# Neighbour search of an adjacency pass: three spans of 683 columns over four load slots in place of four pieces of 512

## Chip, cores and metric

One Trainium2 chip, one core. The metric is the device time of one execution in microseconds; lower is better. Three runs of the kernel before gave 4296.23, 4297.94 and 4300.20 us, median 4297.94 us. The rows below come from one more execution, taken with the profiler.

## What is computed

Four graph layers over `x` (8192 nodes, 128 features) and `adj` (8192 x 8192 float32, 256 MiB, mostly zeros: each row has a one on its own diagonal place and about eight other entries). Cut to what matters:

```
h = relu(layernorm(x));  x += relu((D^-1 A') h W0^T + b0)          # layer 0, A' from adj and alpha
h = relu(layernorm(x));  x += hyperbolic layer on adj, W1           # layer 1
h = relu(layernorm(x));  hh = h W2^T + b2                           # layer 2
                         x += max over the 32 largest entries of each row of adj of hh
h = relu(layernorm(x));  x += hyperbolic layer on adj, W3, b3       # layer 3
```

Layer 2 needs, for every row of `adj`, the columns of its 32 largest entries. A row has far fewer than 32 positive entries, so the list is all its positive columns and then the lowest-numbered zero columns.

## The kernel before, in words

The kernel reads `adj` once in its own layout. That is the adjacency pass, 16 groups (`g`) of 512 rows, each group 16 pieces (`c`) of 512 columns. A piece is 128 partitions x 4 rows x 512 columns, 1 MB, and goes to one of four slots of the SBUF tensor `PIECES`, slot `c % 4`. Each piece has three readers, on three engines:

- **TensorE (PE)** transposes it (line 526), in two pairs of 128-column blocks per piece, 32 pairs (`k`) in a group, and multiplies the transposed pair with `H` for layer 0 (line 539).
- **ScalarE (ACT)** copies each transposed pair from PSUM to one of four buffers `ATS` (line 725), and sums the piece's rows into `rs_part` (line 736). Before the first such sum of a group it waits for `rs_reduced` (line 729), which VectorE tells after its reduction of the group before.
- **VectorE (DVE)** searches it for neighbours (lines 1092 to 1106). For each of the four rows `r` the instruction `max` (MAX8) finds the eight largest values and `max_index` (a MATCH_VALUE_LOAD and a FIND_INDEX8) their places. After the 16 pieces `pick` (lines 1027 to 1086) makes of the 16 x 8 candidates of a row two lists, the near one (columns under 2048, the first four pieces) and the far one, and `L1113` adds up the row sums. If the eighth candidate of any piece is above zero, a row may have more than the search found, and line 1067 marks its tile for a slow general form, which searches the whole row again.

GpSimd's queue (POOL) stores each transposed pair, 512 KB, to the DRAM tensor `adj_turned` (line 420), so that the later layers can read the matrix transposed; pair `k` goes out after its copy and at most three stores are under way, as line 422 waits for the store two before.

The order of the loads is set by SyncE's queue (lines 323 to 332). For each piece in order it waits until the slot's old piece has been transposed (`pair_transposed`), searched (`piece_scanned`) and summed (`piece_summed`), and then issues the load (line 331). All loads of the pass stand in this one queue, in order, and each reader waits for its own slot's `piece_loaded`. The counter `piece_scanned` is raised by every MAX8 and every FIND_INDEX8, eight times per piece (`SCAN`).

After the pass come the layers 1 to 3 on the transposed copy, with gathers for layer 2 by the near and far lists (lines 433 and following). They take the same lists and the same row sums whatever way the search was made.

Of the kernel before, what the change touches and what calls it, by code (L numbers as in the profile page):

```python
# [5 lines left out]
TPG = 4  # L6
GROUP = TPG * P
PIECE = 512
SLOTS = 4
TOPK = 32  # L10
PREFIX = 64
NEAR = 4
# [17 lines left out]
ALU = mybir.AluOpType  # L30
ACT = mybir.ActivationFunctionType
AX = mybir.AxisListType
# [41 lines left out]
def build(nc, x, adj, alpha, w0, b0, w1, w2, b2, w3, b3, out):  # L74
# [3 lines left out]
    NPC = N // PIECE  # L78
    BPP = PIECE // P
    NP = NT // 2  # L80
    K4 = NPC // SLOTS
    NSG = NG // SGG
    TSG = TPG * SGG
    SGW = GROUP * SGG
# [18 lines left out]
    with ctx:  # L103
# [6 lines left out]
        def sem(name):  # L110
# [6 lines left out]
        PIECES = sb("PIECES", [P, max(SLOTS * TPG * PIECE, N)])  # L117
# [30 lines left out]
        s4 = sb("s4", [P, 10, TPG])  # L148
# [9 lines left out]
        tsc = sb("tsc", [P, 2, 6])  # L158
        eps_col = sb("eps_col", [P, 1])

        pieces = [PIECES[:, i * TPG * PIECE:(i + 1) * TPG * PIECE].rearrange("p (r x) -> p r x", r=TPG)
                  for i in range(SLOTS)]
        slot_v = [PIECES[:, i * 2 * SGW:(i + 1) * 2 * SGW].rearrange("p (b h x) -> p b h x", b=2, h=SGG)
                  for i in range(SLOTS)]
        wide = [PIECES[:, i * 2 * SGW:(i + 1) * 2 * SGW].rearrange("p (b x) -> p b x", b=2) for i in range(SLOTS)]
# [7 lines left out]
        ACC = AGG[:, :, :].rearrange("p (s r) f -> p s (r f)", r=TSG)  # L173
        DOT = H[:, :, :].rearrange("p (s r) f -> p s (r f)", r=TSG)

        CW = NPC * 8
        at = [0]

        def part(n):
# [3 lines left out]

        cand = part(TPG * CW).rearrange("p (r c e) -> p r c e", r=TPG, e=8)
        cidx = part(TPG * CW).bitcast(u32).rearrange("p (r c e) -> p r c e", r=TPG, e=8)
        cbase = part(TPG * CW).rearrange("p (r c e) -> p r c e", r=TPG, e=8)
        pos = part(TPG * CW).rearrange("p (r c e) -> p r c e", r=TPG, e=8)
        keys = part(TPG * CW).rearrange("p (r k) -> p r k", r=TPG)
        zero = part(TPG * PREFIX).rearrange("p (r k) -> p r k", r=TPG)
# [29 lines left out]
        piece_scanned = sem("piece_scanned")  # L219
# [72 lines left out]
        HALF = [slice(0, NT // 2), slice(NT // 2, NT)]  # L292
        PICK = 11 + 13 * TPG
        SCAN = 2 * TPG
        FULL_A = 16 * (1 + HALFK)
        FULL_B = 16 * HALFK
        PIECES_L1 = NSG * NP

# [14 lines left out]
        def _(sp):  # L313
# [9 lines left out]
            with sp.Fori(0, NG) as g:  # L323
                for c in range(NPC):
                    sp.wait_ge(pair_transposed, g * (2 * NPC) + 2 * (c + 1))
                    sp.sem_inc(carrier["sp"], 1)
                    sp.wait_ge(piece_scanned, g * (NPC * SCAN) + SCAN * (c + 1))
                    sp.sem_inc(carrier["sp"], 1)
                    sp.wait_ge(piece_summed, g * NPC + (c + 1))
                    sp.sem_inc(carrier["sp"], 1)  # L330
                    sp.dma_start(pieces[c % SLOTS], adj_v[bass.ds(g, 1), c, :, :, :])\
                      .then_inc(piece_loaded[c % SLOTS], 16)
# [44 lines left out]
            for c in range(CHUNKS):  # L377
                for s in range(NSG):
                    for kk in range(2):
                        n = (c * NSG + s) * 2 + kk  # L380
# [13 lines left out]
        def _(pool):  # L394
# [10 lines left out]

            pool.wait_ge(pass_ready, 1)
            pool.memset(ones, 1.0).then_inc(pick_constants, 1)
            pool.iota(cbase, [[0, TPG], [PIECE, NPC], [0, 8]], base=1, channel_multiplier=0,
                      allow_small_or_imprecise_dtypes=True).then_inc(pick_constants, 1)

            pool.sem_inc(pair_free, NAT)
# [521 lines left out]
        def _(dve):  # L933
            v = nc.vector
# [92 lines left out]
            def pick(g):  # L1027
                cf = [a.rearrange("p r c e -> p (r c e)") for a in (cand, cidx, cbase, pos)]
                kf = keys.rearrange("p r k -> p (r k)")
                posk = pos.rearrange("p r c e -> p r (c e)")  # L1030
                near, far = slice(0, NEAR * 8), slice(NEAR * 8, CW)
                lists = ((near, 0), (far, HALFK))
                pk.mark(v.tensor_tensor(kf, cf[1], cf[2], ALU.add))
                pk.mark(v.tensor_scalar(cf[3], cf[0], 0.0, None, ALU.is_gt))
# [52 lines left out]

            def scan_pass():
                with dve.Fori(0, NG) as g:
                    sc.enter(g, SCAN * NPC)  # L1090
                    pk.enter(g, PICK)
                    for c in range(NPC):
                        dve.wait_ge(piece_loaded[c % SLOTS], g * (16 * K4) + 16 * (c // SLOTS + 1))
                        dve.sem_inc(carrier["dve"], 1)
                        pc = pieces[c % SLOTS]
                        if c == 0:
                            pk.mark(v.tensor_scalar(zero, pc[:, :, 0:PREFIX], 0.0, None, ALU.is_equal))
                            pk.mark(v.tensor_reduce(s4[:, 6, :], pc[:, :, 0:PREFIX], AX.X, ALU.min))
                            pk.settle()
                        found = []  # L1100
                        for r in range(TPG + 1):
                            if r < TPG:
                                found.append(sc.mark(v.max(cand[:, r, c, :], pc[:, r, :])))  # L1103
                            if r:
                                sc.settle(found[r - 1])
                                sc.mark(v.max_index(cidx[:, r - 1, c, :], cand[:, r - 1, c, :], pc[:, r - 1, :]))  # L1106
                    sc.settle()
                    dve.wait_ge(pick_constants, 2)
                    pick(g)

                    dve.wait_ge(piece_summed, g * NPC + (NPC + SLOTS))
                    dve.sem_inc(carrier["dve"], 1)
                    pk.mark(v.tensor_reduce(tiles_of(RS[:, :], g), rs_part[:, :, :], AX.X, ALU.add))  # L1113
                    pk.settle(tell=rs_reduced)
                sc.leave(NG)
                pk.leave(NG)
# [249 lines left out]

            sc = Steps(dve, piece_scanned, carrier["dve"])
            pk = Steps(dve, pick_step, carrier["dve"])
            dve.sem_inc(piece_scanned, SCAN * SLOTS)
            dve.sem_inc(rs_reduced, 1)  # L1370
            dve.sem_inc(row_used, 1)
            link(v.memset(ones_col[:, :], 1.0))
            link(v.memset(eps_col[:, :], LN_EPS))
            sc.base = SCAN * SLOTS
            dve.wait_ge(s_load, LOADS)
            dve.wait_ge(ident_ready, 2)
            dve.wait_ge(extra_constants, 3)
# [154 lines left out]
```

## Time and profile before

| what | us |
|---|---|
| median of three runs | 4297.94 |
| lowest, highest | 4296.23, 4300.20 |
| the profiled execution, its time | 4298.19 |
| its span in the trace | 4296.5 |
| DVE busy in the span | 3633.9 (85%) |
| PE busy | 3459.1 (81%) |
| ACT busy | 1676.9 (39%) |
| POOL busy | 1639.1 (38%) |
| first search of the pass starts, last group's search starts | 91.6, 1588.9 |

The span is what the trace covers; the execution's own time is 1.7 us longer. A busy time is the sum of an engine's instructions with overlaps counted once. In the lines by group, "busy, mean ns" is followed by the idle time of the engine before these instructions and by what ended it. Durations of neighbouring VectorE instructions overlap by some tens of ns, so the pitch from start to start is shorter than the duration.

### The profile page before, as it was taken

Reading aid. Unit: us, or ns where it says so; the run is one execution under the profiler, and the core shown is the slowest. Engines: PE = TensorE matmul, PEld = TensorE weight load, DVE = VectorE, ACT = ScalarE, POOL = GpSimd, SP = SyncE. Lnnn points to the kernel's source line nnn. Section 1 sums busy time; section 2 is a strip of 40 time slices with the busy share of each in tenths; the row PEclk is TensorE's granted clock in tenths of the full one; section 3 lists DMA queues with packets and bytes.
Section 4 is the critical chain, followed back from the end, with each engine's and each line's share of the span. In section 5 each row is a group of like instructions: output and inputs, shape, how many; then the busy total and the mean of one; then the engine's idle time right before and its main releaser. Section 6 shows DMA issues by size and latency. Waiting matters only on the chain.

```text
span 4296.5 us, 52828 instructions
## 1 busy us (share of the span) xinstructions
PE 3459.1 (81%) x11588; PEld 1809.8 (42%) x11588; DVE 3633.9 (85%) x6461; ACT 1676.9 (39%) x4239; POOL 1639.1 (38%) x1850
## 2 busy tenths in 40 slices
PE   3988888898888985289998898870688978888883
PEld 3555555555555553234443343430233433333343
DVE  6999999999999999777777888882689999999964
ACT  2777777777767774300210302222111111111134
POOL 0111111111111111000037677764777777777600
PEclk9999999999999997689999999985799989999985
DMA  3988988998888985168788798881688888888841
GB/s 113 347 345 333 348 340 341 342 344 340 335 323 323 333 339 209 39 236 298 268 311 296 270 335 285 295 278 38 194 282 303 308 290 293 297 300 297 297 163 39
DMA packets 569318, 1189.00 MB, mean 277 GB/s; under 512 B 45133, under 2 KB 87054, under 8 KB 569038
## 3 DMA queue, kind: packets, MB, share of 16 engines
q1 hardware_dynamic: 426160, 818.40, 53.7%
q0 software_dynamic: 116096, 355.32, 22.5%
q10 hardware_dynamic: 26782, 12.62, 1.0%
q14 instruction: 237, 1.94, 0.1%
q8 instruction: 43, 0.70, 0.1%
HBM read 905.12 MB, written 281.05 MB: 276 GB/s over the span
## 4 chain that ended last, share of the span: by engine, by line
DVE 40%; issue 25%; POOL 13%; PE 12%; DMA 4%; ACT 3%; DVEq 2%; POOLq 1%; SPq 0%; ACTq 0%
POOL D L433 13%; DVE D L1103 12%; PE psT L600 7%; DVE D L1106 6%; DVE H L1354 4%; DMA D<-h_table,idx_now 4%; DVE ATS L1329 2%; DVE gmax L1150 2%; DVE AGG L1365 1%; PE psT L654 1%; ACT junk_rows L754 1%; DVEq L56 1%; DVE D L1052 1%; DVE sm L977 1%; DVE D L1057 1%
## 5 line engine op out<-in xcount | busy, mean ns | idle before, releaser
L433 POOL DMA_INDIRECT D<-h_table,idx_now x1324 | 1362.4, 1029 | 1022.6 <-issue 972.8
L539 PE MATMUL psU<-ATS,H 128*128 128x512 f32 x2048 | 1006.8, 617 | 123.7 <-ACT ATS L725 123.6
L600 PE MATMUL psT<-PIECES,H 128*128 128x512 f32 x2048 | 926.6, 611 | 88.1 <-DMA PIECES<-adj_turned 55.9
L654 PE MATMUL psT<-PIECES,ATS 128*128 128x512 f32 x1376 | 640.8, 621 | 191.3 <-ACT ATS L842 155.4
L420 POOL DMA_DIRECT2D adj_turned<-ATS x512 | 272.6, 532 | 1303.6 <-ACT ATS L725 846.3
L1106 DVE FIND_INDEX8 D<-D,PIECES 128x8 uint32<-128x512 f32 x1024 | 695.6, 686 | 0.0
L1329 DVE SCALAR_TENSOR_TENSOR ATS<-PIECES,dots,ATS 128x1024 f32<-128x1024 f32 x496 | 611.6, 1286 | 82.6 <-DMA PIECES<-adj_turned 75.6
L1103 DVE MAX8 D<-PIECES 128x8 f32<-128x512 f32 x1024 | 670.6, 676 | 2.3
L1354 DVE SCALAR_TENSOR_TENSOR H<-PIECES,DINV,H 128x1024 f32<-128x1024 f32 x504 | 647.4, 1287 | 29.6 <-DMA PIECES<-adj_turned 7.4
L600 PEld LDWEIGHTS psT<-PIECES,H 128*128 128x128 f32 x2048 | 393.8, 196 | 595.0 <-issue 459.1
L725 ACT ACTIVATE ATS<-psT 128x1024 f32<-128x1024 f32 x512 | 520.4, 1023 | 312.7 <-PE psT L526 162.1
L526 PEld LDWEIGHTS psT<-ident,PIECES 128*128 128x128 f32 x4096 | 488.5, 144 | 307.5 <-issue 232.8
L526 PE MATMUL psT<-ident,PIECES 128*128 128x128 f32 x4096 | 545.1, 278 | 27.8 <-DMA PIECES<-in_adj 26.2
L539 PEld LDWEIGHTS psU<-ATS,H 128*128 128x128 f32 x2048 | 362.0, 197 | 398.9 <-issue 337.4
L654 PEld LDWEIGHTS psT<-PIECES,ATS 128*128 128x128 f32 x1376 | 268.7, 199 | 545.4 <-issue 359.7
L654 PE MATMUL psU<-PIECES,ATS 128*128 128x512 f32 x672 | 317.0, 625 | 63.2 <-ACT ATS L842 32.3
L736 ACT ACTIVATE psX<-PIECES 128x512 f32<-128x512 f32 x512 | 303.6, 593 | 82.6 <-DVEq L58 82.6
L1150 DVE TENSOR_REDUCE gmax<-D 128x128 f32<-128x1664 f32 (+3 forms) x64 | 207.7, 3245 | 127.0 <-DMA D<-h_table,idx_now 126.2
L736 ACT ACTIVATE psY<-PIECES 128x512 f32<-128x512 f32 x512 | 301.3, 588 | 0.0
L842 ACT ACTIVATE ATS<-xc,tsc 128x128 f32<-128x128 f32 x64 | 25.7, 402 | 579.1 <-DVE tsc L1208 579.1
L654 PEld LDWEIGHTS psU<-PIECES,ATS 128*128 128x128 f32 x672 | 132.9, 202 | 236.4 <-issue 188.9
L761 ACT ACTIVATE ATS<-psT 128x1024 f32<-128x1024 f32 x8 | 8.2, 1023 | 489.8 <-PE psT L600 489.0
(268 smaller groups left out, 2197.5 us busy)
## 6 DMA issues: line engine op xcount, KB each, us to landing
PIECES<-adj_turned SPq DMA_DIRECT2D x512, 1024.0 KB
PIECES<-in_adj SPq DMA_DIRECT2D x256, 1024.0 KB
adj_turned<-ATS POOLq DMA_DIRECT2D x512, 512.0 KB, 6.7
D<-h_table,idx_now POOLq DMA_INDIRECT x1324
base_rows<-GB SPq DMA_DIRECT2D x64, 64.0 KB
D<-base_rows ACTq DMA_DIRECT2D x64, 64.0 KB
D<-h_table ACTq DMA_DIRECT2D x64, 64.0 KB
out_x<-X SPq DMA_DIRECT2D x2, 2048.0 KB, 8.7
```

Source lines behind the costliest of these rows:

```text
L433: pool.indirect_dma_start(ring[par][:, slot, :], None, near_table if done is near_gathered else table, bass.IndirectOffsetOnAxis(ap=idx_no ...
L526: last = nc.tensor.transpose(psT[k % 2][:, b * GROUP + r * P:b * GROUP + (r + 1) * P], pieces[(k // 2) % SLOTS][:, r, x0:x0 + P], ident[:, :])
L539: last = nc.tensor.matmul(psA, H[:, j, :], AT[k % NAT][:, b * GROUP:(b + 1) * GROUP], start=(j == 0), stop=(j == NT - 1))
L600: last = nc.tensor.matmul(psT[s % 2][:, h * GROUP:(h + 1) * GROUP], H[:, j, :], wide[q % SLOTS][:, b, h * GROUP:(h + 1) * GROUP], start=(j ...
L654: last = nc.tensor.matmul(acc[:, h * GROUP:(h + 1) * GROUP], Hc[c % 2][:, jj, :], wide[q % SLOTS][:, b, h * GROUP:(h + 1) * GROUP], start= ...
L725: nc.scalar.activation(AT[k % NAT], psT[k % 2][:, :], ACT.Copy).then_inc(pair_copied, 1)
L736: st.mark(nc.scalar.activation(junk[r % 2][:, :], pieces[c % SLOTS][:, r, :], ACT.Copy, accum_out=rs_part[:, r, c:c + 1]))
L1103: found.append(sc.mark(v.max(cand[:, r, c, :], pc[:, r, :])))
L1106: sc.mark(v.max_index(cidx[:, r - 1, c, :], cand[:, r - 1, c, :], pc[:, r - 1, :]))
L1150: v.tensor_reduce(out, ring[par][:, 0:cuts[0] + 1, :].rearrange("p k f -> p f k"), AX.X, ALU.max).then_inc(done, 1)
L1329: last[b] = d2.mark(v.scalar_tensor_tensor(dacc[b], piece, scale, dacc[b], ALU.mult, ALU.add))
L1354: d2.mark(v.scalar_tensor_tensor(DOT[:, s, :], piece, scale, DOT[:, s, :], ALU.mult, ALU.add))
```

## The change

The four slots of `PIECES` are laid out so that the four rows of 2048 columns are each contiguous across the slots: slot `i` is columns 512i to 512i+511 of every row. The loads, the transposes and the sums still go by pieces of 512. The search goes by three spans per four slots, columns 0 to 682, 683 to 1365 and 1366 to 2047. The first span reads slots 0 and 1, the second slots 1 and 2, the third slots 2 and 3. VectorE therefore searches nothing when slot 0 has landed, and one span after each of the slots 1, 2 and 3. SyncE reloads slot 0 after the first span, slot 1 after the second, and slots 2 and 3 both after the third (`min(c % SLOTS, NCUT - 1)`). A row has 12 x 8 candidates in place of 16 x 8, so the arrays that `pick` works on hold 384 elements per partition in place of 512; the near list comes from three spans. GpSimd's `iota` of the base columns follows the cuts.

```diff
--- before.py
+++ after.py
@@ -79,6 +79,9 @@
     BPP = PIECE // P
     NP = NT // 2
     K4 = NPC // SLOTS
+    CUTS = [0, 683, 1366, SLOTS * PIECE]
+    NCUT = len(CUTS) - 1
+    NSC = K4 * NCUT
     NSG = NG // SGG
     TSG = TPG * SGG
     SGW = GROUP * SGG
@@ -158,8 +161,9 @@
         tsc = sb("tsc", [P, 2, 6])
         eps_col = sb("eps_col", [P, 1])
 
-        pieces = [PIECES[:, i * TPG * PIECE:(i + 1) * TPG * PIECE].rearrange("p (r x) -> p r x", r=TPG)
-                  for i in range(SLOTS)]
+        rows_v = PIECES[:, 0:SLOTS * TPG * PIECE].rearrange("p (r x) -> p r x", r=TPG)
+        pieces = [rows_v[:, :, i * PIECE:(i + 1) * PIECE] for i in range(SLOTS)]
+        spans = [rows_v[:, :, a:b] for a, b in zip(CUTS, CUTS[1:])]
         slot_v = [PIECES[:, i * 2 * SGW:(i + 1) * 2 * SGW].rearrange("p (b h x) -> p b h x", b=2, h=SGG)
                   for i in range(SLOTS)]
         wide = [PIECES[:, i * 2 * SGW:(i + 1) * 2 * SGW].rearrange("p (b x) -> p b x", b=2) for i in range(SLOTS)]
@@ -173,7 +177,7 @@
         ACC = AGG[:, :, :].rearrange("p (s r) f -> p s (r f)", r=TSG)
         DOT = H[:, :, :].rearrange("p (s r) f -> p s (r f)", r=TSG)
 
-        CW = NPC * 8
+        CW = NSC * 8
         at = [0]
 
         def part(n):
@@ -292,6 +296,7 @@
         HALF = [slice(0, NT // 2), slice(NT // 2, NT)]
         PICK = 11 + 13 * TPG
         SCAN = 2 * TPG
+        NEAR_SCANS = NCUT * NEAR // SLOTS
         FULL_A = 16 * (1 + HALFK)
         FULL_B = 16 * HALFK
         PIECES_L1 = NSG * NP
@@ -324,7 +329,7 @@
                 for c in range(NPC):
                     sp.wait_ge(pair_transposed, g * (2 * NPC) + 2 * (c + 1))
                     sp.sem_inc(carrier["sp"], 1)
-                    sp.wait_ge(piece_scanned, g * (NPC * SCAN) + SCAN * (c + 1))
+                    sp.wait_ge(piece_scanned, g * (NSC * SCAN) + SCAN * (c // SLOTS * NCUT + min(c % SLOTS, NCUT - 1) + 1))
                     sp.sem_inc(carrier["sp"], 1)
                     sp.wait_ge(piece_summed, g * NPC + (c + 1))
                     sp.sem_inc(carrier["sp"], 1)
@@ -405,7 +410,8 @@
 
             pool.wait_ge(pass_ready, 1)
             pool.memset(ones, 1.0).then_inc(pick_constants, 1)
-            pool.iota(cbase, [[0, TPG], [PIECE, NPC], [0, 8]], base=1, channel_multiplier=0,
+            pool.iota(cbase.rearrange("p r (i n) e -> p r i n e", n=NCUT),
+                      [[0, TPG], [SLOTS * PIECE, K4], [CUTS[1], NCUT], [0, 8]], base=1, channel_multiplier=0,
                       allow_small_or_imprecise_dtypes=True).then_inc(pick_constants, 1)
 
             pool.sem_inc(pair_free, NAT)
@@ -1028,7 +1034,7 @@
                 cf = [a.rearrange("p r c e -> p (r c e)") for a in (cand, cidx, cbase, pos)]
                 kf = keys.rearrange("p r k -> p (r k)")
                 posk = pos.rearrange("p r c e -> p r (c e)")
-                near, far = slice(0, NEAR * 8), slice(NEAR * 8, CW)
+                near, far = slice(0, NEAR_SCANS * 8), slice(NEAR_SCANS * 8, CW)
                 lists = ((near, 0), (far, HALFK))
                 pk.mark(v.tensor_tensor(kf, cf[1], cf[2], ALU.add))
                 pk.mark(v.tensor_scalar(cf[3], cf[0], 0.0, None, ALU.is_gt))
@@ -1087,23 +1093,26 @@
 
             def scan_pass():
                 with dve.Fori(0, NG) as g:
-                    sc.enter(g, SCAN * NPC)
+                    sc.enter(g, SCAN * NSC)
                     pk.enter(g, PICK)
                     for c in range(NPC):
                         dve.wait_ge(piece_loaded[c % SLOTS], g * (16 * K4) + 16 * (c // SLOTS + 1))
                         dve.sem_inc(carrier["dve"], 1)
-                        pc = pieces[c % SLOTS]
                         if c == 0:
-                            pk.mark(v.tensor_scalar(zero, pc[:, :, 0:PREFIX], 0.0, None, ALU.is_equal))
-                            pk.mark(v.tensor_reduce(s4[:, 6, :], pc[:, :, 0:PREFIX], AX.X, ALU.min))
+                            pk.mark(v.tensor_scalar(zero, pieces[0][:, :, 0:PREFIX], 0.0, None, ALU.is_equal))
+                            pk.mark(v.tensor_reduce(s4[:, 6, :], pieces[0][:, :, 0:PREFIX], AX.X, ALU.min))
                             pk.settle()
+                        if c % SLOTS == 0:
+                            continue
+                        n = c // SLOTS * NCUT + c % SLOTS - 1
+                        span = spans[c % SLOTS - 1]
                         found = []
                         for r in range(TPG + 1):
                             if r < TPG:
-                                found.append(sc.mark(v.max(cand[:, r, c, :], pc[:, r, :])))
+                                found.append(sc.mark(v.max(cand[:, r, n, :], span[:, r, :])))
                             if r:
                                 sc.settle(found[r - 1])
-                                sc.mark(v.max_index(cidx[:, r - 1, c, :], cand[:, r - 1, c, :], pc[:, r - 1, :]))
+                                sc.mark(v.max_index(cidx[:, r - 1, n, :], cand[:, r - 1, n, :], span[:, r - 1, :]))
                     sc.settle()
                     dve.wait_ge(pick_constants, 2)
                     pick(g)
@@ -1366,12 +1375,12 @@
 
             sc = Steps(dve, piece_scanned, carrier["dve"])
             pk = Steps(dve, pick_step, carrier["dve"])
-            dve.sem_inc(piece_scanned, SCAN * SLOTS)
+            dve.sem_inc(piece_scanned, SCAN * NCUT)
             dve.sem_inc(rs_reduced, 1)
             dve.sem_inc(row_used, 1)
             link(v.memset(ones_col[:, :], 1.0))
             link(v.memset(eps_col[:, :], LN_EPS))
-            sc.base = SCAN * SLOTS
+            sc.base = SCAN * NCUT
             dve.wait_ge(s_load, LOADS)
             dve.wait_ge(ident_ready, 2)
             dve.wait_ge(extra_constants, 3)
```

## Rows read from the trace of the kernel before

**Rows 1.** Page, busy time by engine and the span in 40 slices.

```profile
PE 3459.1 (81%) x11588; PEld 1809.8 (42%) x11588; DVE 3633.9 (85%) x6461; ACT 1676.9 (39%) x4239; POOL 1639.1 (38%) x1850
...
DVE  6999999999999999777777888882689999999964
...
DMA  3988988998888985168788798881688888888841
```

**Rows 2.** The instructions of line 1097, one per group: durations, first and last start.

```profile
L1097 DVE TENSOR_SCALAR D<-PIECES x16: 294/294/976, 91.6 to 1588.9; 128x256 f32<-128x256 f32 x16
```

**Rows 3.** Groups of instructions, whole span: busy us, mean ns, idle before.

```profile
L1106 DVE FIND_INDEX8 D<-D,PIECES 128x8 uint32<-128x512 f32 x1024 | 695.6, 686 | 0.0
...
L1103 DVE MAX8 D<-PIECES 128x8 f32<-128x512 f32 x1024 | 670.6, 676 | 2.3
```

**Rows 4.** VectorE in order of time, one group: start us, length, instruction.

```profile
392.08 0.29 DVE L1097 TENSOR_SCALAR D<-PIECES 128x256 f32<-128x256 f32 x1 [3.25 <-issue]
...
392.85 1.29 DVE L1103 MAX8 D<-PIECES 128x8 f32<-128x512 f32 x2
...
468.07 1.27 DVE L1103 MAX8 D<-PIECES 128x8 f32<-128x512 f32 x2
```

**Rows 5.** Waits of VectorE, 91 to 1680 us: total, times, longest.

```profile
DVE D L1097 <- issue: 50.8, 15, 4.2
```

**Rows 6.** Windows: length, busy of PE, PEld, DVE, ACT, POOL, PEclk, DMA share, GB/s.

```profile
400.00:480.00 80.00, 73.76 (x333) 43.60 (x331) 79.26 (x202) 62.71 (x141) 14.46 (x28) 1.00 1.01 369
...
430.00:435.00 5.00, 5.00 (x24) 2.99 (x24) 5.00 (x13) 4.31 (x11) 0.63 (x2) 1.00 1.03 414
...
485.00:490.00 5.00, 3.29 (x5) 1.45 (x6) 2.30 (x16) 3.14 (x6) 1.06 (x2) 0.66 0.35 138
```

**Rows 7.** SyncE's load issues in order of time, same group.

```profile
398.34 0.37 SPq L331 DMA_DIRECT2D PIECES<-in_adj  x1
...
403.35 0.37 SPq L331 DMA_DIRECT2D PIECES<-in_adj  x1
...
408.54 0.37 SPq L331 DMA_DIRECT2D PIECES<-in_adj  x1
...
423.41 0.37 SPq L331 DMA_DIRECT2D PIECES<-in_adj  x1
...
451.28 0.37 SPq L331 DMA_DIRECT2D PIECES<-in_adj  x1
```

**Rows 8.** TensorE's weight loads that waited for a load, same group, then a later one.

```profile
412.24 0.85 PEld L526 LDWEIGHTS psT<-ident,PIECES 128*128 128x128 f32 x8 [0.63 <-DMA PIECES<-in_adj]
...
419.29 0.74 PEld L526 LDWEIGHTS psT<-ident,PIECES 128*128 128x128 f32 x7 [2.47 <-DMA PIECES<-in_adj]
...
435.80 0.86 PEld L526 LDWEIGHTS psT<-ident,PIECES 128*128 128x128 f32 x8 [0.60 <-DMA PIECES<-in_adj]
...
718.53 0.86 PEld L526 LDWEIGHTS psT<-ident,PIECES 128*128 128x128 f32 x8 [1.19 <-DMA PIECES<-in_adj]
...
734.00 0.14 PEld L526 LDWEIGHTS psT<-ident,PIECES 128*128 128x128 f32 x1 [0.31 <-DMA PIECES<-in_adj]
```

**Rows 9.** TensorE's transposes in order of time, one pair each.

```profile
412.28 1.06 PE L526 MATMUL psT<-ident,PIECES 128*128 128x128 f32 x8
...
414.89 1.04 PE L526 MATMUL psT<-ident,PIECES 128*128 128x128 f32 x8
...
472.30 1.04 PE L526 MATMUL psT<-ident,PIECES 128*128 128x128 f32 x8
```

**Rows 10.** Groups of VectorE instructions by shape, to 1700 us.

```profile
L1052 DVE MAX8 D<-D 128x8 f32<-128x96 f32 x128 | 31.5, 246 | 3.0 <-issue 3.0
L1052 DVE MAX8 D<-D 128x8 f32<-128x32 f32 x128 | 23.1, 180 | 2.3
...
L1038 DVE TENSOR_REDUCE s<-D 128x4 f32<-128x512 f32 x16 | 10.9, 678 | 0.0
...
L963 DVE TENSOR_REDUCE sm<-X 128x64 f32<-128x8192 f32 x1 | 8.7, 8686 | 0.0
```

## Prediction

> **What bounds the kernel now.** I read the slices of the page first [rows 1]: VectorE stands at 9 in the first 40% of the span, and the DMA engines at 8 or 9 beside it. That stretch is the adjacency pass. The change touches nothing outside it but the contents of the same lists, so the question is the length of one group, 16 times. Line 1097 starts once per group, first at 91.6 and last at 1588.9 us [rows 2]; 15 periods make (1588.9 - 91.6)/15 = 99.82 us each.
>
> Then VectorE in order of time [rows 4]. A group's search starts at 392.85 us and a new piece starts every 5.015 us ((468.07 - 392.85)/15). Sixteen pieces take 80.2 us, and the other 19.6 us are the pick, a gap of 3.3 us before line 1097, and its prefix work. In the whole pass VectorE waits for nothing that matters except that gap of 50.8 us in 15 times [rows 5]. It never waits for a load. By these rows VectorE is the bound, and an instruction taken from it shortens the pass.
>
> The third view, the windows [rows 6], says how near the next limit is. From 400 to 480 us, the search of one group, the DMA engines are busy 1.01 of the time and move 369 GB/s. From 485 to 490 they are at 0.35: all four slots are full and VectorE picks. So during the search the transfers are already at their limit and only the gap lets them catch up. What lets VectorE run without waits is that a slot is released three pieces, 3 x 5.0 = 15.0 us, before it is needed again.
>
> How much of those 15 us is used is the figure I need, and TensorE gives it, since it waits at times for a load [rows 8]. The last transposed pair of the group (number 31) starts at 472.30; the pair that starts at 412.28 is 21 back, number 10, the first of piece 5 [rows 9]. So piece 5 landed at about 412.2; its load was issued at 403.35 [rows 7]: 8.9 us. Piece 6 landed at 419.3 and was issued at 408.54: 10.8 us. Piece 9 landed at 435.8, issued at 423.41: 12.4 us, 2.2 us before VectorE wanted it (392.85 + 9 x 5.015 = 438.0). The load of piece 4, issued at 398.34 onto an empty queue, is bounded from above by TensorE's pair 8, two pairs of 2.6 us before pair 10: at most 8.4 us with its issue. A megabyte lands every (435.8 - 412.2)/4 = 5.9 us here, and every 5.2 us in a later group (718.5 to 734.0 in three loads, pieces 6 to 9) [rows 8].
>
> **The change, part by part.**
>
> The search itself. Its columns stay 2048 per four slots; 16 of 64 pairs of MAX8 and FIND_INDEX8 a group go. A row's pair takes 5.015/4 = 1.254 us from start to start. The cost of a column comes from reductions of 512 and 8192 columns, (8686 - 678)/7680 = 1.043 ns [rows 10], which also fits the durations of both searches at 512 [rows 3]: 534 ns of columns and about 150 of fixed cost. With 171 more columns twice, a pair takes 1.254 + 2 x 0.178 = 1.611 us, a span of four rows 6.44 us, twelve spans 77.3 us. Against 80.2 that is -2.9 us a group.
>
> The pick. The arrays shrink by a quarter. Three full operations at one column per step (lines 1033, 1037, 1038) lose 128 columns each, 0.40 us; two at half that cost (1034, 1047) 0.13; line 1043 loses 4 x 32, 0.13; lines 1035, 1060, 1061 together 0.15; sixteen MAX8 of line 1052 lose 8 (near) or 24 (far) columns each, on durations of 180 and 246 ns at 32 and 96 columns [rows 10], 0.27; line 1057 loses 0.13. Sum -1.2 us a group. Nothing hides this: ScalarE waits for the end of the pick too.
>
> The iota, the counters and the slice of the near list cost nothing in the loop: the iota is one instruction before the pass, and SyncE still makes three waits and one issue per piece. The new layout leaves the load's runs at 512 columns, 2 KB, in DRAM, and the transposes and sums read the same shapes. I take 0 for it. The bounds for a row layout with an 8 KB pitch in SBUF, which no row shows, are -0.5 and +0.5 us a megabyte, a tenth of 5.2; the shapes that move are the same, so I take the middle.
>
> If VectorE stayed the bound these two would give 99.8 - 4.1 = 95.7 us a group, -66 us.
>
> **What is moved: the waits.** A span needs two slots, and releases are coarser. Per round of four slots, with span ends at 6.44, 12.9 and 19.3 us: slot 0 is released at 6.44 and needed at 19.3; slot 1 is released at 12.9 and needed at 19.3, since the next round's first span reads it; slot 2 is released at 19.3 and needed 6.44 later; slot 3 is released at the same time and needed 12.9 later. The margin falls from 15.0 us to 6.44 for half of the loads. Every latency above is over 6.44. From either short loop a round can't be shorter than the two spans between need and release plus the load: 12.9 + 0.4 (the issue) + latency. At 8.4 us that is 21.7 us a round, against 20.06 before and 19.3 wanted.
>
> Now one group step by step, from its search start, with 5.2 us per queued load. Before, piece 4 was issued at 5.5 and piece 5 landed at 19.4. Now piece 4 is issued at 6.9, 1.4 later, so piece 5 lands at about 20.8, where VectorE was ready at 19.3. The loads of 6 and 7 go out at 19.8 and queue behind it; 7 lands near 34, in time. 8 lands near 39, 9 near 44.2. Round 2 needs 9 and would have started at 40.1: a wait of 4. Four more loads of 5.2 put piece 13 at 65.0 and round 3 with it. Round 3 has its loads in time and ends 19.3 us later, at 84.5. Before it was 80.2. The rest of the group is 19.6 - 1.2 = 18.4 us. Together 102.9 us against 99.8: +3.1 us a group, 16 groups +49 us. At 5.9 us per load the third round starts near 69 and the group takes 107 (+115 us in all). At 5.05 us, half of the fastest rate of the windows (414 GB/s [rows 6], two streams), with piece 5 at 20.3, it starts at 60.7 and the group takes 98.4 (-23 us). I take 5.2, because it comes from the group in the middle of the pass; the group at 392 with 5.9 has the same period.
>
> What is late next: TensorE needs 2.6 us a pair (412.28 to 414.89) [rows 9], 5.2 a piece, so it isn't faster than the loads, and its lag holds slots too. Piece 14's load went out at 451.28 although VectorE had left that slot (piece 10) at 392.85 + 11 x 5.015 = 448.0. This keeps the upper side open.
>
> A rule to weigh here: the Trainium skill, page "DMA: Bandwidth & Descriptors", section "Anatomy of one DMA", gives a transfer as 2.0 us plus its bytes over 436 GB/s. As an estimate by it a load of 1 MB takes 4.4 us, fits the 6.44 us, and the change would gain its full 66 us. The trace doesn't agree: 8.9 to 12.4 us beside the stores.
>
> **The sum** against the profiled execution's own 4298.2 us (0.3 above the median of 4297.9): -66 for VectorE's work, +115 for waits that take its place, 4346 us.
>
> **Rivals.**
>
> *Full gain.* Loads alone are quicker than those I could see, because fewer are in flight at once, and VectorE stays without waits: 4298 - 66 = 4232 us. It decides at a latency of 6.4 us. For it: the DMA engines rest in the gap, and queueing is part of the 12.4 us. Against it: even the load onto a nearly empty queue took up to 8.4 us, stores run beside it, and 8.39 MB per round at 369 GB/s take 22.7 us where VectorE wants 19.3. 10%.
>
> *Part of the gain.* TensorE gets its pieces later, stores thin out, loads get more than half, near 5.05 us each: -23 us or somewhat better, 4255 to 4289. 14%.
>
> *No change.* The bytes decide: 33.5 MB a group and the idle stretch at its end stay, VectorE's gain becomes waiting in the same amount. 4290 to 4307. 10%.
>
> *Much slower.* The queue stays as deep as at piece 9, 12.4 us: rounds of 25.7 us, three of them 6.4 longer than 19.3, a group of 115 us, about 4540; above 4420 8%.
>
> *It isn't what it says.* A row with eight entries in one span would go to the general form. I counted the reference's own adjacency: the most in any span of the new cuts is 7 (6 in the pieces of 512), so no tile is marked, and the lists are as before.
>
> **Chances.** The forecast, slower by 0.2 to 2.8%, has 58%. Slower in all 66%, faster 24% (the first two rivals), within 0.2% (9 us, about what a measurement of this kernel can tell) 10%. The range leaves out the full gain and the much slower case: 4262 to 4420. The likeliest case alone spans 4307 to 4420.
>
> **What would show it.** In the trace after: MAX8 near 854 ns on 683 columns, 768 of them; pick operations on 384. For the waits: VectorE idle before line 1103 with a load of PIECES as releaser, about 7 us a group, at the first span of rounds 1, 2 and 3, largest in round 2; hardly any at third spans. A period of line 1097 near 102.9. DMA share in the search near 1.0 and GB/s unchanged. TensorE waiting for loads more often. I'm wrong if VectorE shows no such waits (then 95.7 a group), if the loads land under 6.4 us after issue, or if the waits sit behind TensorE or ScalarE as the last to release a slot.

## The result, and the profile after

The changed kernel took 4388.82 us in the median of four runs (4384.13 to 4391.96), the kernel before 4297.08 (4293.84 to 4300.20). The ratio is 1.0213, 95% interval 1.0195 to 1.0230: slower by 92 us. The forecast was 4346 us, 48 us slower, with 4420 us as the upper end.

| | before | after |
|---|---|---|
| profiled execution, us | 4298.19 | 4391.26 |
| its span, us | 4296.5 | 4389.5 |
| period of a group, us | 99.82 | 105.87 |
| VectorE waits for loads in the pass, us | 0 | 157.3 |
| DMA rate, 200 to 1600 us, GB/s | 337 | 317 |

The page of the changed kernel, busy time and the lines that answer to [rows 1, 3] (busy us, mean ns, idle before and what ended it):

```profile
PE 3478.1 (79%) x11588; PEld 1803.3 (41%) x11588; DVE 3572.8 (81%) x5693; ACT 1677.8 (38%) x4239; POOL 1643.9 (37%) x1850
...
L1112 DVE MAX8 D<-PIECES 128x8 f32<-128x683 f32 (+1 forms) x768 | 641.2, 856 | 161.6 <-DMA PIECES<-in_adj 157.3
...
L1115 DVE FIND_INDEX8 D<-D,PIECES 128x8 uint32<-128x683 f32 (+1 forms) x768 | 658.7, 864 | 0.0
```

VectorE is busy 61 us less (the forecast took off 66, counted from start to start). MAX8 on 683 columns takes 856 ns (forecast 854). In front of it, where 2.3 us of idle time stood and no wait for a load, stand 161.6 us, and loads of `PIECES` ended 157.3 of them. Line 1102 is the old line 1097, once per group; beside [rows 2] it stands as:

```profile
L1102 DVE TENSOR_SCALAR D<-PIECES x16: 293/294/810, 92.0 to 1680.0; 128x256 f32<-128x256 f32 x16
```

(1680.0 - 92.0)/15 = 105.87 us. The account closes: 99.8 of before, minus 4.1 of VectorE's work, plus 161.6/16 = 10.1 of waits, makes 105.8. Sixteen groups of 6.05 us are 97 us; the whole execution is 93.1 us longer.

The pick's operations on the smaller arrays, in the groups by shape to 1800 us, against [rows 10]:

```profile
L1058 DVE MAX8 D<-D 128x8 f32<-128x72 f32 x128 | 28.0, 219 | 0.0
L1058 DVE MAX8 D<-D 128x8 f32<-128x24 f32 x128 | 22.0, 172 | 2.3
L1039 DVE TENSOR_TENSOR D<-D 128x384 f32<-128x384 uint32 x16 | 8.9, 558 | 2.4
L1044 DVE TENSOR_REDUCE s<-D 128x4 f32<-128x384 f32 x16 | 8.7, 546 | 0.0
```

Where the waits stand shows in VectorE's order of time, one group from its start (all its waits for loads):

```profile
835.47 0.29 DVE L1102 TENSOR_SCALAR D<-PIECES 128x256 f32<-128x256 f32 x1 [4.03 <-issue]
...
836.35 1.64 DVE L1112 MAX8 D<-PIECES 128x8 f32<-128x683 f32 x2 [0.26 <-DVE s L1103]
...
857.71 1.64 DVE L1112 MAX8 D<-PIECES 128x8 f32<-128x683 f32 x2 [1.95 <-DMA PIECES<-in_adj]
...
864.96 1.65 DVE L1112 MAX8 D<-PIECES 128x8 f32<-128x683 f32 x2 [0.71 <-DMA PIECES<-in_adj]
...
880.24 1.64 DVE L1112 MAX8 D<-PIECES 128x8 f32<-128x683 f32 x2 [2.31 <-DMA PIECES<-in_adj]
...
887.80 1.64 DVE L1112 MAX8 D<-PIECES 128x8 f32<-128x683 f32 x2 [1.01 <-DMA PIECES<-in_adj]
...
904.62 1.64 DVE L1112 MAX8 D<-PIECES 128x8 f32<-128x683 f32 x2 [3.85 <-DMA PIECES<-in_adj]
```

Counted from the search start at 836.35: 21.4, 28.6, 43.9, 51.5 and 68.3 us. These are the first and second spans of rounds 1 and 2 and the first span of round 3, and nothing before a third span. One group isn't the mean: over all 16 groups, the waits for loads before the first spans of rounds 1, 2 and 3 add up to 49.1, 45.6 and 48.2 us, those before the second spans of these rounds to 14.4, and there is none before a third span. A first span waits for slot 1, a second for slot 2, the two slots with the short margin. SyncE's issues of the loads that ended three of these waits (pieces 5, 9 and 13):

```profile
849.70 0.37 SPq L336 DMA_DIRECT2D PIECES<-in_adj  x1
...
871.88 0.37 SPq L336 DMA_DIRECT2D PIECES<-in_adj  x1
...
894.71 0.37 SPq L336 DMA_DIRECT2D PIECES<-in_adj  x1
```

They took 8.0, 8.4 and 9.9 us from issue to the end of the wait, each above the 6.44 us that the release leaves. Over all 16 groups the loads of pieces 5, 9 and 13 took 9.0 us in the mean, 7.9 to 11.3. And they were issued as soon as VectorE let go, 0.4 us after the end of its last FIND_INDEX8. SyncE's own waits, 200 to 1600 us (total, times, longest), first of the changed kernel:

```profile
SPq L333 <- DVE D L1115: 1181.6, 159, 22.0
SPq L331 <- PE psT L532: 21.9, 18, 2.4
```

then of the kernel before:

```profile
SPq L328 <- DVE D L1106: 1078.3, 222, 22.3
SPq L326 <- PE psT L526: 70.9, 63, 4.8
SPq L330 <- ACTq L58: 33.0, 26, 4.4
```

Before, TensorE and ScalarE were at times the last to release a slot; now it is nearly always VectorE's span. The window of the search from 844 to 914 us, in the columns of [rows 6]:

```profile
844.00:914.00 70.00, 61.50 (x278) 36.07 (x277) 60.18 (x112) 51.73 (x116) 11.96 (x23) 1.00 0.99 345
```

The DMA engines are as full as before (0.99, before 1.01), and move 345 GB/s where they moved 369. Such short windows depend on where they are laid: over a whole search (392 to 473 us before, 836 to 924 after) the share is 0.95 in both kernels and the rates are 345 before and 334 after. From 200 to 1600 us the shares are 0.89 and 0.90, the rates 337 and 317.

### The profile page after: what moved, and what is told of

It is laid out like the page before. It is cut to its first block, busy times and chain, and to the rows that moved or that the text cites. A ratio compares the mean times of both kernels' runs of the same rounds, so it can differ in the third digit from the quotient of the medians.

```text
span 4389.5 us, 51484 instructions
## 1 busy us (share of the span) xinstructions
PE 3478.1 (79%) x11588; PEld 1803.3 (41%) x11588; DVE 3572.8 (81%) x5693; ACT 1677.8 (38%) x4239; POOL 1643.9 (37%) x1850
## 4 chain that ended last, share of the span: by engine, by line
DVE 31%; issue 23%; DMA 15%; POOL 13%; PE 11%; ACT 3%; DVEq 2%; POOLq 1%; SPq 1%; ACTq 0%
POOL D L439 13%; DMA PIECES<-in_adj 11%; PE psT L606 7%; DVE D L1112 7%; DVE H L1363 4%; DVE D L1115 4%; DMA D<-h_table,idx_now 3%; DVE ATS L1338 2%; DVE gmax L1159 2%; PE psT L660 1%; ACT junk_rows L760 1%; DVE AGG L1374 1%; DVE sm L983 1%; DVE D L1058 1%; DVE D L1063 1%
## 5 line engine op out<-in xcount | busy, mean ns | idle before, releaser
L1112 DVE MAX8 D<-PIECES 128x8 f32<-128x683 f32 (+1 forms) x768 | 641.2, 856 | 161.6 <-DMA PIECES<-in_adj 157.3
L731 ACT ACTIVATE ATS<-psT 128x1024 f32<-128x1024 f32 x512 | 521.2, 1024 | 424.7 <-PE psT L532 267.3
L1115 DVE FIND_INDEX8 D<-D,PIECES 128x8 uint32<-128x683 f32 (+1 forms) x768 | 658.7, 864 | 0.0
L1159 DVE TENSOR_REDUCE GB<-D 128x128 f32<-128x896 f32 (+2 forms) x64 | 114.9, 1796 | 99.6 <-DMA D<-h_table,idx_now 85.0
```

The lines of the kernel that those rows point to most:

```text
L731: nc.scalar.activation(AT[k % NAT], psT[k % 2][:, :], ACT.Copy).then_inc(pair_copied, 1)
L1112: found.append(sc.mark(v.max(cand[:, r, n, :], span[:, r, :])))
L1115: sc.mark(v.max_index(cidx[:, r - 1, n, :], cand[:, r - 1, n, :], span[:, r - 1, :]))
L1159: v.tensor_reduce(out, ring[par][:, 0:cuts[0] + 1, :].rearrange("p k f -> p f k"), AX.X, ALU.max).then_inc(done, 1)
```

## Experiments

Two things in this profile needed telling apart. The coarse release explains waits (the release theory). But the engines moved fewer bytes while full, and the new layout of the slots, which I had costed at nothing, could be the cause (the layout theory). Runs in one table or paragraph share a chip. On the chip of e1 to e3 and on that of e6 to e9 the kernel before took 4703 and 4666 us: the layers after the pass were 370 to 400 us longer there, while the pass was not (e1's groups below have the length of [rows 2]). So groups are compared by their period, times by the ratio to the kernel before on the same chip.

**e1, the layout alone**

```diff
-        pieces = [PIECES[:, i * TPG * PIECE:(i + 1) * TPG * PIECE].rearrange("p (r x) -> p r x", r=TPG)
-                  for i in range(SLOTS)]
+        rows_v = PIECES[:, 0:SLOTS * TPG * PIECE].rearrange("p (r x) -> p r x", r=TPG)
+        pieces = [rows_v[:, :, i * PIECE:(i + 1) * PIECE] for i in range(SLOTS)]
```

> The kernel before with one part of the change alone: the four slots laid out as rows of 2048 columns, so that a load writes four runs of 2 KB at a pitch of 8 KB; search, release and pick as before. Release theory (all of the loss comes from the coarser release of slots, the layout costs nothing): 4298 us within 9 us, 99.8 us a group. Layout theory (in the trace of the changed kernel the loads' queue took 49.9% of 16 engines for 221 MB, before 47.6% for 236 MB, so 12% more engine time a megabyte, about 5.4 us a group, and this comes from the layout): the margin of 2 us at piece 9 is used up and VectorE waits for loads, 101 to 105 us a group, 4315 to 4380 us.

Measured: ratio 0.9988 [0.9955, 1.0020].

```profile
L1097 DVE TENSOR_SCALAR D<-PIECES x16: 293/294/978, 92.2 to 1589.4; 128x256 f32<-128x256 f32 x16
200.00:1600.00 1400.00, 1249.92 (x5445) 744.49 (x5444) 1315.93 (x3694) 1024.67 (x2271) 239.53 (x449) 0.95 0.90 337
```

99.81 us a group and 337 GB/s, both as before. The layout costs nothing that shows.

**e2, the new search on the old layout**

```diff
-        spans = [rows_v[:, :, a:b] for a, b in zip(CUTS, CUTS[1:])]
+        spans = [PIECES[:, TPG * a:TPG * b].rearrange("p (r x) -> p r x", r=TPG) for a, b in zip(CUTS, CUTS[1:])]
...
-                pk.mark(v.tensor_tensor(tiles_of(FLAGS[:, 2, :], g), s4[:, 4, :], s4[:, 5, :], ALU.max))
+                pk.mark(v.tensor_tensor(tiles_of(FLAGS[:, 2, :], g), s4[:, 4, :], s4[:, 4, :], ALU.subtract))
```

Left out of the cut is the layout of `pieces`, which is the old one again.

> The changed kernel with the old layout of the slots. Each span reads 683 columns that lie one behind the other in the old layout, with the same two slots under it and so the same waits and releases; it finds other columns than the rows', so lists and output are others, and the mark for the general form is held at zero. Release theory: as the changed kernel, 105.9 us a group, near 4389 us. Layout theory: the loads take their old engine time, a load lands every 5.2 us as I forecast, 102 to 103 us a group, 4330 to 4350 us. If under 99.8 us a group, the release costs less than VectorE gains, and the layout alone made the change slower.

```profile
L1102 DVE TENSOR_SCALAR D<-PIECES x16: 293/294/809, 92.2 to 1673.8; 128x256 f32<-128x256 f32 x16
200.00:1600.00 1400.00, 1194.98 (x5148) 701.77 (x5149) 1194.22 (x2844) 968.90 (x2150) 225.99 (x426) 0.95 0.90 319
DVE D L1112 <- DMA PIECES<-in_adj: 147.3, 62, 4.6
```

The groups (line 1102), the window and VectorE's wait for loads (to 1700 us; the changed kernel has 149.3 there): 105.44 us a group, 319 GB/s. The old layout gives back 0.4 us of 6. The lower rate belongs to the release, not to the layout. The whole took 5017 us, a ratio of 1.067, but its lists are other ones, so only its pass is read.

**e3, rows padded to a pitch of 8448 bytes**

```diff
+PAD = 64
...
-        rows_v = PIECES[:, 0:SLOTS * TPG * PIECE].rearrange("p (r x) -> p r x", r=TPG)
+        rows_v = PIECES[:, 0:TPG * (SLOTS * PIECE + PAD)].rearrange("p (r x) -> p r x", r=TPG)
```

> The changed kernel with 64 columns between the rows, a pitch of 8448 bytes in place of 8192. If it is the round pitch that makes the loads dearer, this comes out as the old layout with spans does. If it is that a load writes four separate runs in place of one, or if the layout costs nothing, it is as the changed kernel, 105.9 us a group, within 9 us of 4389.

```profile
L1103 DVE TENSOR_SCALAR D<-PIECES x16: 293/294/811, 92.4 to 1682.4; 128x256 f32<-128x256 f32 x16
```

106.0 us a group, ratio 1.0226 [1.0127, 1.0325]. So 64 columns more of pitch change nothing that shows. With e1 and e2 the layout theory falls.

**e4 and e5, small stores in the kernel before and in the changed one**

```diff
-                    pool.dma_start(turned[bass.ds(g, 1), k, :, :], AT[k % NAT]).then_inc(pair_stored[k % NAT], 16)
+                    pool.dma_start(turned[bass.ds(g, 1), k, :, 0:P], AT[k % NAT][:, 0:P]).then_inc(pair_stored[k % NAT], 16)
...
-                sp.dma_start(slot_v[q % SLOTS], turned_v[s, k, :, :, :, :]).then_inc(piece_loaded[q % SLOTS], 16)
+                sp.dma_start(PIECES[:, i * 2 * SGW:(i + 1) * 2 * SGW].rearrange("p (r x) -> p r x", r=TPG),
+                             adj_v[2 * s + k // NPC, k % NPC, :, :, :]).then_inc(piece_loaded[q % SLOTS], 16)
```

> The kernel before with the transposed stores of the pass cut from 512 KB to 64 KB each, and the later layers reading adj itself in place of the transposed copy (so their input is another). Tells what the pass is without the stores beside it. If VectorE bounds the pass before: 99.8 us a group as with the stores.

> The changed kernel with the same small stores. My theory: the spans' release leaves a load 6.4 us, and only the stores beside it make it take longer; without them VectorE has next to no waits and the group falls to the 95.7 us that its own work takes. Rival (a load of 1 MB takes over 6.4 us with its issue even alone): waits stay, 98 us or more.

One run each: 4301.1 us for e4, 4246.3 for e5, beside 4315.4 for the kernel before. First e4's line of the groups:

```profile
L1099 DVE TENSOR_SCALAR D<-PIECES x16: 293/294/975, 91.1 to 1587.0; 128x256 f32<-128x256 f32 x16
```

then e5's, with its wait for loads (91 to 1700 us):

```profile
L1104 DVE TENSOR_SCALAR D<-PIECES x16: 293/294/811, 91.3 to 1531.1; 128x256 f32<-128x256 f32 x16
DVE D L1114 <- DMA PIECES<-in_adj: 4.3, 10, 1.2
```

and the loads of e4 and of e5 from 200 to 1600 us, with the median from issue to landing at the end:

```profile
PIECES<-in_adj SPq DMA_DIRECT2D x225, 1024.0 KB, 5.4
PIECES<-in_adj SPq DMA_DIRECT2D x235, 1024.0 KB, 6.3
```

e4 has 99.73 us a group: VectorE really was the bound before, large stores or small. e5 has 95.99, which is the 95.7 of VectorE's own work (with the gap before line 1104) and 0.3 of waits. A megabyte beside small stores fits the 6.4 us; it is the large stores beside it that make it too late. This is also where the Trainium skill's rule that I weighed would have been good enough (page "DMA: Bandwidth & Descriptors", section "Anatomy of one DMA"): it gives an estimated 4.4 us for 1 MB. The page states it for transfers that GpSimd issues, and SyncE issues these loads. The trace without the large stores has 5.4 us in e4, 1.0 more than the rule and still inside the margin; the changed kernel's has 9.0 beside them.

**e7 and e8, other cuts.** The number of instructions and columns is equal; only margins move.

```diff
-    CUTS = [0, 683, 1366, SLOTS * PIECE]
+    CUTS = [0, 512, 1280, SLOTS * PIECE]      # e7;  e8: [0, 512, 1024, SLOTS * PIECE]
...
+    LAST = [max(n for n in range(NCUT) if CUTS[n] < (i + 1) * PIECE) for i in range(SLOTS)]
+    READY = [-(-CUTS[n + 1] // PIECE) - 1 for n in range(NCUT)]
```

`LAST` is the last span that reads a slot, for which SyncE waits; `READY` is the slot whose load lets a span start. The base columns follow the cuts (left out here).

> The changed kernel with cuts at 512 and 1280 (spans of 512, 768, 768 columns): as much work of VectorE and as many instructions. By the margins: slot 0 has 14.3 us, slots 1 and 3 have 12.2, slot 2 alone has 5.0, as it is released with the third span and needed by the second. Release theory: VectorE waits for loads before second spans, 3 us or more a time in three to four rounds, and hardly before first spans; the round is 14.3 + 0.4 + 8, 22 to 23 us, the group 103 to 107. Bytes theory: the waits move with the queue, not with the cuts, and stand before first spans too.

> Cuts at 512 and 1024 (spans of 512, 512, 1024 columns). No span begins or ends inside a slot. Slots 0 and 1 have a margin of 14.3 us, slots 2 and 3 are released together and both needed 10.0 us later, where a first load takes 8 us and the next 5.3 more. Release theory: waits before third spans of about 3 us, the group 102 to 106 us. If a load's latency were hidden by the longer margin, 96 to 99 us, faster than the kernel before.

The first instruction of one group of e7, and every wait for a load behind it to 927 us:

```profile
849.75 0.29 DVE L1105 TENSOR_SCALAR D<-PIECES 128x256 f32<-128x256 f32 x1 [3.39 <-issue]
...
878.16 1.82 DVE L1115 MAX8 D<-PIECES 128x8 f32<-128x768 f32 x2 [3.23 <-DMA PIECES<-in_adj]
...
901.68 1.82 DVE L1115 MAX8 D<-PIECES 128x8 f32<-128x768 f32 x2 [4.11 <-DMA PIECES<-in_adj]
...
926.79 1.82 DVE L1115 MAX8 D<-PIECES 128x8 f32<-128x768 f32 x2 [5.70 <-DMA PIECES<-in_adj]
```

and one of e8:

```profile
889.77 2.35 DVE L1115 MAX8 D<-PIECES 128x8 f32<-128x1024 f32 x2 [5.23 <-DMA PIECES<-in_adj]
...
913.32 2.35 DVE L1115 MAX8 D<-PIECES 128x8 f32<-128x1024 f32 x2 [4.13 <-DMA PIECES<-in_adj]
...
938.64 2.35 DVE L1115 MAX8 D<-PIECES 128x8 f32<-128x1024 f32 x2 [5.92 <-DMA PIECES<-in_adj]
```

In e7 all waits for loads stand before second spans, in e8 all before third ones (1024 columns), 48 in the 16 groups of each, and none where the changed kernel had its largest, before first spans of rounds. The waits follow the margins, which a queue full of bytes alone wouldn't do. The groups are 108.1 and 109.5 us (lines 1105: 91.5 to 1713.4 and 91.1 to 1733.2), one microsecond above what I had expected for e7 and 3.5 above for e8. In e8's group shown, the third spans started 14.7, 13.8 and 15.6 us after the issue of the first of the two loads that go out together, where I had counted 8 and 5.3. e7, run once, took 4791.1 us. e8's ratio is 1.0311 [1.0254, 1.0367], slower than the changed kernel, though no span crosses a slot but the long one.

**e6, and again e11: loads by rows.** The changed kernel, each slot's load in four, one per row. The wait for the search stands behind the two others, one for each row (3, 5, 7, 8 are the counts at which the rows' searches have ended), and all who wait for a slot of the pass count to 64 in place of 16.

```diff
-                    sp.wait_ge(piece_scanned, g * (NSC * SCAN) + SCAN * (c // SLOTS * NCUT + min(c % SLOTS, NCUT - 1) + 1))
-                    sp.dma_start(pieces[c % SLOTS], adj_v[bass.ds(g, 1), c, :, :, :])\
-                      .then_inc(piece_loaded[c % SLOTS], 16)
...
+                    for r, done in enumerate((3, 5, 7, 8)):
+                        sp.wait_ge(piece_scanned, g * (NSC * SCAN) + SCAN * (c // SLOTS * NCUT + min(c % SLOTS, NCUT - 1)) + done)
+                        sp.dma_start(pieces[c % SLOTS][:, r, :], adj_v[bass.ds(g, 1), c, :, r, :])\
+                          .then_inc(piece_loaded[c % SLOTS], 16)
```

> The changed kernel with each load of a slot split into its four rows, 256 KB each; a row's load waits for the search of that row alone, so three quarters of a slot's reload can start before the span ends. Release theory (a span's slots come back 6.4 us before they are needed, and a megabyte takes 8 us): only the last 256 KB have the short margin, waits of VectorE for loads fall from 10 us a group to under 4, the group to 97 to 101 us, 90 to 30 us of time off the changed kernel. Rival, the bytes decide (the DMA engines are full and mixed traffic gives only 345 GB/s): 105.9 us a group as in the changed kernel, or more for the smaller transfers.

e6 had 98.83 us a group (91.1 to 1573.6) and a ratio of 0.9969 [0.9936, 1.0003] to the kernel before: most of the loss was gone, the sign open. So it ran again, with the changed kernel beside it.

> The changed kernel with loads by rows once more, the same kernel as e6_row_loads, against the kernel before and the two kernels below on one chip. By e6's trace a group is 98.83 us where the kernel before has 99.82: 16 groups make 16 us less than before, a ratio of 0.996, if nothing after the pass moves.

> The changed kernel as it is, on the same chip as the loads by rows. 105.9 us a group, about 92 us over the kernel before of this chip; 108 us over the loads by rows.

The groups, the window from 200 to 1600 us and VectorE's wait for loads of e11:

```profile
L1103 DVE TENSOR_SCALAR D<-PIECES x16: 293/294/809, 92.1 to 1570.8; 128x256 f32<-128x256 f32 x16
200.00:1600.00 1400.00, 1252.86 (x5528) 745.24 (x5527) 1276.82 (x3052) 1040.25 (x2309) 241.78 (x455) 0.97 0.91 342
DVE D L1113 <- DMA PIECES<-in_adj: 48.9, 28, 3.7
```

| same chip | median us | ratio to before | group us |
|---|---|---|---|
| before | 4291.92 | | |
| e12, changed | 4388.87 | 1.0230 [1.0216, 1.0244] | 105.7 |
| e11, changed, loads by rows | 4273.06 | 0.9962 [0.9950, 0.9975] | 98.58 |

The same search with the earlier reload is 116 us faster than the change and faster than the kernel before. VectorE's 95.7 us and 48.9/16 = 3.1 of waits make 98.8. This undoes the loss by changing only when the loads may start and in what sizes. A changed kernel with loads by rows that all wait for the whole span was not run, so the 116 us aren't divided between the two; e10 tests the sizes where nothing waits.

**e10, loads by rows in the kernel before.** The same edit of lines 323 to 332 there, and of the waits for a slot.

> The kernel before with loads by rows. Its VectorE never waits for a load, so an earlier reload has nothing to give: 99.8 us a group, no change within 9 us. Rival: quarter loads are themselves a gain or a loss (more issues, shorter queues), and then this moves as well, and e6's gain over the kernel before is not the search's.

4293.28 us, ratio 1.0005 [0.9994, 1.0016]:

```profile
L1098 DVE TENSOR_SCALAR D<-PIECES x16: 294/294/975, 91.4 to 1586.8; 128x256 f32<-128x256 f32 x16
```

99.7 us a group. Quarter loads are neither gain nor loss where the margin is 15 us. The Trainium skill (page "DMA: Bandwidth & Descriptors", section "Bandwidth") advises transfers of 1 MiB or more; beside a busy queue these runs show no price for 256 KB (338 GB/s from 200 to 1600 us, before 337).

**e9, both: cuts at 512 and 1024, loads by rows**

```diff
-    CUTS = [0, 683, 1366, SLOTS * PIECE]
+    CUTS = [0, 512, 1024, SLOTS * PIECE]
```

> Cuts at 512 and 1024 together with the loads by rows. Slot 2's rows are released 2.7 us apart while the long span runs, and its reload begins 8 us earlier; slot 3 keeps 10 us. Release theory: this takes away nearly all waits, VectorE's own work of 95.7 us a group shows, or the DMA engines' limit of about 97; 4235 to 4280 us where the kernel before takes 4298, faster than both. Bytes theory: 100 us a group or more.

A miss: 101.6 us a group (90.9 to 1614.6), ratio 1.0024 [0.9991, 1.0057]. It is 8 us better than e8, but waits of up to 5.9 us before third spans remain. Slot 3's rows go out only behind slot 2's in SyncE's one queue, and in this kernel SyncE spent 287.8 us of 1400 waiting for ScalarE (196.6 in e6). Which of the two holds the third span wasn't tried.

## Why the prediction was right, and what was mis-sized

**VectorE's gain: right.** The forecast 95.7 us a group came out as 95.99 in e5 with 0.3 of waits in it, MAX8 at 856 ns for 854, and the pick as counted (line 1044 takes 132 ns less than the old line 1038, by the forecast's cost of a column 133.5).

**The wait that takes its place: right in mechanism, and mostly in place.** The waits are for loads that the coarser release starts late, and nine tenths of them stand before first spans. e7 and e8 moved the waits with the margins, e11 took two thirds of them away, e5 nearly all. Three signs were missed. "Largest in round 2" is wrong: the working had 1.5, 4.1 and 1.5 us in rounds 1, 2 and 3, and the first spans waited 3.1, 2.9 and 3.0 in the mean. Second spans wait too, 0.9 us a group. And the rate is not unchanged (317 GB/s for 337). TensorE does wait more for loads, as forecast (its weight loads 181.1 us for 65.8, from 200 to 1600 us).

**Its size: too small.** I put 7.2 us of waits a group (115 us in all); it was 10.1 (161.6). By steps, from the search start, measured in the mean of 16 groups:

| | forecast us | measured us |
|---|---|---|
| round 1 starts | 20.8 | 22.5 |
| round 2 starts | 44.2 | 44.9 |
| round 3 starts | 65.0 | 67.9 |
| the search ends | 84.5 | 87.7 |

The step that failed is the length of a round by a count of queued loads, 20.8 us for rounds 0 and 2 ("Four more loads of 5.2 put piece 13 at 65.0"); they took 22.5 and 23.1. The prediction held the better rule and didn't apply it: a round can't be shorter than 12.9 + 0.4 + latency, 21.7 us even at 8.4. With the 9.0 us that these loads took it gives 22.3. Round 2's good place is two errors that cancel: round 0 was 1.7 us longer than I had put, round 1 (22.4 for 23.4) 1.0 shorter.

One group shows what the count left out. TensorE's weight loads after a load, around piece 13 in the changed kernel:

```profile
880.15 0.14 PEld L532 LDWEIGHTS psT<-ident,PIECES 128*128 128x128 f32 x1 [0.34 <-DMA PIECES<-in_adj]
887.70 0.85 PEld L532 LDWEIGHTS psT<-ident,PIECES 128*128 128x128 f32 x8 [2.70 <-DMA PIECES<-in_adj]
893.24 0.85 PEld L532 LDWEIGHTS psT<-ident,PIECES 128*128 128x128 f32 x8 [0.96 <-DMA PIECES<-in_adj]
899.24 0.85 PEld L532 LDWEIGHTS psT<-ident,PIECES 128*128 128x128 f32 x8 [1.42 <-DMA PIECES<-in_adj]
```

Piece 9 lands at 880.15, 10 at 887.7, 11 at 893.2, 12 at 899.2, and 13 ended VectorE's wait at 904.6. The load of piece 10, issued at 878.31 when the one before had 1.8 us to go, took 7.6 us after it; the others 5.5, 6.0 and 5.4. The sum for round 3 counts all four as queued at 5.2. A load whose slot comes back late finds a nearly empty queue, and here that cost some 2 us. From piece 5 (857.7) to 13 the mean is 5.86 us, near the 5.9 that I had read in one group and set aside for the 5.2 of another. That value would have given 4413 us; the truth lay between.

**Where luck helped.** The three values of the range weren't worked alike. At 5.05 us piece 13 is put eight loads after piece 5 (20.3 + 8 x 5.05 = 60.7), at 5.2 it comes 2.6 us later than eight loads, as the way to round 2 is 23.4 us and not 20.8. Worked as the first, the likely case has round 3 at 62.4 and a group of 100.1 us, next to no change. So the sign came out of 2.6 us that the count itself doesn't hold. What decides is the loop: three rounds of 20.7 us, the last of 19.3 and the rest of 18.4 make the 99.8 us of before, so a load above 7.4 us (20.7 - 12.9 - 0.4) means a loss. The rows had 8.9 to 12.4, and at most 8.4 onto an empty queue. Smaller slips: 65.0 + 19.3 is 84.3 and not 84.5, the sum gives 4347 and not 4346, and the 8.4 us of piece 4's load are without its issue (with it 8.7).

**The layout: right at nothing** (e1, 99.81; e2 bounds it at 0.4 us a group).

**The rivals.** The full gain fell because the loads beside the stores took too long: of the 68 that VectorE waited for, none had been issued less than 7.9 us before. "The bytes decide" fell too: with the same bytes a group took 105.9 to 109.5 us by the cuts alone, and 98.6 with loads by rows.

## What to carry to other kernels

A buffer's margin, from its release to its next use, is a cost to be priced like work: list it per buffer before and after, beside the load's measured time under that kernel's own traffic, and take the load that starts on an empty queue, not the queued one. Margin and load close a loop whose length is a lower bound; hold every step-by-step count against it. Fewer, longer instructions on the bounding engine release their inputs in larger lumps; if the transfers were close to late, split the reload so that it follows the reader row by row.

## What the runs showed that I had not expected

The DMA engines' time for a megabyte of loads is not a constant. From the queues' shares of 16 engines over 200 to 1600 us (share x 22400 / MB): before 45.2 us, changed 50.6, the old layout with spans 50.7, loads by rows (e11) 44.7, and with small stores (e4) 54.3. The shares, in the kernel before, the changed one, e11 and e4:

```profile
q1 hardware_dynamic: 118768, 235.89, 47.6%
```

```profile
q1 hardware_dynamic: 111147, 220.76, 49.9%
```

```profile
q1 hardware_dynamic: 131144, 238.79, 47.7%
```

```profile
q1 hardware_dynamic: 118772, 235.89, 57.2%
```

The stores stayed at 39 to 41 us a megabyte where they were large. Loads cost 44 to 46 us where slots come back one by one or row by row, 49 to 52 where two come back at once, and 51 to 54 beside small stores (51.5 in e5). So a DMA share of 0.95 over a search stood for 334 GB/s in one kernel and 345 in the other, and the share alone doesn't tell how much room is left. What in the engines makes this difference no run here separates.
